# In the loop over pairs of routed tiles, VectorE loads its table behind the products and copies the turned intermediate ahead of the weight copies

## The reference, cut to what matters

```python
# first layer: 32 experts, 4 per token, inner size 192, softmax over the 4 chosen, times 1.8
g = silu(einsum('th,eih->tei', xf, gate_w)); u = einsum('th,eih->tei', xf, up_w)
routed = einsum('tei,ehi,te->th', g * u, down_w, combine)
shared = silu(xf @ shared_gate_w.T) * (xf @ shared_up_w.T) @ shared_down_w.T
# second layer: 8 experts, 2 per token, inner size 176, softmax over all 8
h = silu(einsum('nc,eic->eni', xf, w1)) * einsum('nc,eic->eni', xf, w2)
y = einsum('enc,ne->nc', einsum('eni,eci->enc', h, w3), comb)
sh = silu(xf @ sw1.T) * (xf @ sw2.T) @ sw3.T
```

## Time and profile before

| | us |
|---|---|
| median of 3 runs | 429.84 (426.48 to 432.18) |
| the profiled execution's own time | 427.56 |
| its span in the profile | 425.8 |
| PE busy | 343.6 (81%) |
| DVE busy | 271.4 (64%) |
| ACT busy | 194.0 (46%) |
| POOL busy | 185.0 (43%) |

### The profile page before, as it was taken

The page is one execution under the profiler, slowest core; times in us unless marked ns, Lnnn a source line. Parts: engine busy times, 40 slices in busy tenths (PEclk is TensorE's granted clock), DMA queues, the critical chain, the costliest instruction groups (busy, mean ns, idle before and its releaser), DMA issues.

```text
span 425.8 us, 8440 instructions
## 1 busy us (share of the span) xinstructions
PE 343.6 (81%) x2392; PEld 194.7 (46%) x2392; DVE 271.4 (64%) x842; ACT 194.0 (46%) x452; POOL 185.0 (43%) x321
## 2 busy tenths in 40 slices
PE   0019699768989899898999869999876698885997
PEld 0019564424444444444444558666553344442455
DVE  2997869313666655666555487999777266565174
ACT  1368453243545444454443036999812454540010
POOL 2000001382767766676653217666600657744100
PEclk9999855997999999999999988999976999999899
DMA  7999999085332322333354387920020223321341
GB/s 236 365 223 363 226 351 255 22 261 161 99 100 77 100 87 90 97 85 94 108 164 155 115 340 254 228 67 2 2 97 3 86 75 100 91 74 47 124 151 49
DMA packets 35038, 59.88 MB, mean 141 GB/s; under 512 B 4178, under 2 KB 23346, under 8 KB 34994
## 3 DMA queue, kind: packets, MB, share of 16 engines
q1 hardware_dynamic: 26850, 40.41, 32.4%
q0 software_dynamic: 6528, 17.83, 13.6%
q10 hardware_dynamic: 1616, 1.11, 0.9%
HBM read 47.28 MB, written 12.06 MB: 139 GB/s over the span
## 4 chain that ended last, share of the span: by engine, by line
PE 39%; DVE 26%; issue 14%; DVEq 9%; DMA 5%; POOL 4%; ACT 3%; SPq 0%; ACTq 0%; POOLq 0%
PE bank L1414 8%; DVEq L946 8%; PE bank L1246 6%; PE bank L1426 5%; DVE xn L956 4%; DVE hT L977 4%; DVE dn L957 3%; PE bank L1477 3%; PE bank L1465 3%; PE bank L1159 2%; PE bank L1385 2%; DMA xg<-m_xn,tab 2%; DVE ysb L990 2%; PE bank L1259 2%; DMA x_sb<-x 2%
## 5 line engine op out<-in xcount | busy, mean ns | idle before, releaser
L1385 PE MATMUL bank<-arena,xT 128*64 x272 | 94.7, 492 | 2.4 <-ACT xT L647 2.4
L515 POOL DMA_INDIRECT xg<-m_xn,tab x68 | 66.5, 977 | 65.9 <-PE bank L1367 30.4
L1387 PE MATMUL bank<-xn,xT 128*64 128x384 f32 (+1 forms) x272 | 94.7, 492 | 0.0
L504 POOL DMA_INDIRECT m_ys<-ysb,dest x68 | 71.3, 1049 | 44.3 <-DVE ysb L990 26.6
L636 ACT ACTIVATE xn<-arena 128x768 f32 (+1 forms) x68 | 56.3, 827 | 20.8 <-issue 20.5
L956 DVE COPY xn<-arena 64x256 f32 (+1 forms) x136 | 35.0, 296 | 37.2 <-issue 36.1
L1385 PEld LDWEIGHTS bank<-arena,xT 128*64 128x64 f32 x272 | 35.0, 139 | 44.5 <-issue 43.6
L1414 PE MATMUL bank<-arena,hT 128*64 x136 | 36.4, 390 | 20.2 <-DVE hT L977 20.2
L990 DVE COPY ysb<-bank 128x256 f32<-128x256 f32 x68 | 25.7, 420 | 40.2 <-PE bank L1428 40.2
L647 ACT ACTIVATE xT<-bank 128x512 f32<-128x512 f32 (+1 forms) x36 | 21.3, 591 | 56.1 <-PE bank L1367 56.1
L654 ACT ACTIVATE sg<-bank 128x192 f32<-128x192 f32 (+1 forms) x71 | 22.7, 320 | 39.8 <-PE bank L1387 34.1
(11 more groups left out here) (196 smaller groups left out, 670.2 us busy)
## 6 DMA issues: line engine op xcount, KB each, us to landing
arena<-w_gu SPq DMA_DIRECT2D x3, 3456.0 KB, 21.9
arena<-m_ys SPq DMA_DIRECT2D x8, 512.0 KB, 5.8
arena<-w_dn SPq DMA_DIRECT2D x6, 576.0 KB, 13.8
arena<-w_gu SPq DMA_DIRECT2D x2, 1408.0 KB
arena<-w_dn SPq DMA_DIRECT2D x3, 864.0 KB, 22.3
m_xn<-xn SPq DMA_DIRECT2D x2, 1024.0 KB, 9.6
arena<-m_ys SPq DMA_DIRECT2D x8, 256.0 KB, 3.8
arena<-w_dn SPq DMA_DIRECT2D x7, 192.0 KB, 9.1
```

What stands on the lines that cost most here:

```text
L504: nc.gpsimd.indirect_dma_start(out=ys_d[L.name], out_offset=bass.IndirectOffsetOnAxis(ap=dest[:, s:s + 1], axis=0), in_=ysb[:, s % BUFS, : ...
L515: nc.gpsimd.indirect_dma_start(out=xg[:, b, :], out_offset=None, in_=xn_d[L.name], in_offset=bass.IndirectOffsetOnAxis(ap=d["tab"][:, s:s ...
L1385: T.matmul(out[0:BLOCK, 0:2 * J2], xT[:, s % 4, c, 0:BLOCK], arena[:, bass.ds(off + c * 2 * J2, 2 * J2)], start=(c == 0), stop=(c == C - 1 ...
L1387: ins = T.matmul(out[BLOCK:P, 0:2 * J2], xT[:, s % 4, c, BLOCK:P], gu2[:, s % 2, cols], start=(c == 0), stop=(c == C - 1), tile_position=( ...
```

## The change

Only VectorE's list and one wait of TensorE's are different. In VectorE's list for a pair, `dn_second(p)` was one step with the table load, the six weight copies and their waits, and stood between the output copies and the copy of the intermediate. Now the table load is a step of its own, `experts_of(p)`, directly behind the two products and ahead of the output copies; the copy of the intermediate follows the output copies, and the six weight copies come last, in another order: the two copies that are 128 rows high first, then the four tails. Their one wait on earlier down products is now for both tiles at once. The semaphore `dn_second` counts the two high copies; a new one, `tails_in`, counts the four tails, and TensorE waits for it ahead of the tail products only.

```diff
-                def dn_second(p):
+                def experts_of(p):
                     if 2 * p >= L.tiles:
+                        return None
+                    return nc.values_load_multi_w_load_instructions(
+                        d["etab"][0:1, 4 * p:4 * p + 4], engines=(mybir.EngineType.DVE,), min_val=0, max_val=top)[1]
+
+                def dn_second(p, offs):
+                    if offs is None:
                         return
-                    _, offs = nc.values_load_multi_w_load_instructions(
-                        d["etab"][0:1, 4 * p:4 * p + 4], engines=(mybir.EngineType.DVE,), min_val=0, max_val=top)
-                    for t in range(2):
-                        s = 2 * p + t
-                        if s >= 2:
-                            dve.wait_ge(m["d_done"], s - 1)
-                        if L is L0 and s == late_tile:
-                            dve.wait_ge(w_late, 2 * LOAD)
+                    if p >= 1:
+                        dve.wait_ge(m["d_done"], 2 * p)
+                    if L is L0 and 2 * p <= late_tile < 2 * p + 2:
+                        dve.wait_ge(w_late, 2 * LOAD)
+                    even, even_second, odd, odd_second = offs
+                    V.tensor_copy(dn2[:, 0, :], arena[:, bass.ds(even_second + L.gu, H)]).then_inc(m["dn_second"], 1)
+                    V.tensor_copy(dn2[:, 1, :], arena[:, bass.ds(odd_second + L.gu, H)]).then_inc(m["dn_second"], 1)
+                    for t, b, off in ((0, 0, even), (0, 1, even_second), (1, 0, odd), (1, 1, odd_second)):
                         r = slice(t * BLOCK, t * BLOCK + L.tail)
-                        for b in range(2):
-                            V.tensor_copy(tails[r, b, :], arena[r, bass.ds(offs[2 * t + b] + L.gu + H, H)])
-                        V.tensor_copy(dn2[:, t, :], arena[:, bass.ds(offs[2 * t + 1] + L.gu, H)]).then_inc(m["dn_second"], 1)
+                        V.tensor_copy(tails[r, b, :], arena[r, bass.ds(off + L.gu + H, H)]).then_inc(m["tails_in"], 1)
...
                         product(s)
+                    offs = experts_of(p)
                     if p >= 1:
                         y_copy(2 * p - 2)
                         y_copy(2 * p - 1)
-                    dn_second(p)
                     ht_copy(p)
+                    dn_second(p, offs)
...
+                    if 2 * p < L.tiles:
+                        pe.wait_ge(m["tails_in"], 4 * (p + 1))
```

More of the change, by code:

```diff
@@ L271, in mk_xattn_ffn @@
             m = {n: sem(f"{L.name}_{n}") for n in (
-                "xn_ready xn_stored rt_T rt_Tsb logits exp_in exp_out onehots t_done xT_copied gu_second dn_second g_done "
+                "xn_ready xn_stored rt_T rt_Tsb logits exp_in exp_out onehots t_done xT_copied gu_second dn_second tails_in g_done "
                 "sg_ready h_ready ht_done hT_copied d_done y_copied ").split()}
```

## The result

The changed kernel takes 401.02 us (median of 4 runs, 398.99 to 402.18) against 428.89 for the kernel before (4 runs); ratio 0.934 with a 95% interval of 0.926 to 0.942. Run again beside later kernels it was at 0.941 (0.936 to 0.946), 400.99 us. The forecast was 406 us with a range of 400 to 413. The profiled execution took 402.18 us with a span of 400.4 (before 427.56 and 425.8).

The account below looks back on a forecast made before the run. TensorE was nearly the bound, losing 0.53 us a plain pair waiting for VectorE's turned intermediate. Gains 14.0 + 5.4 + 2.0 + 1.6 = 23.0 take 427.56 to 404.6; median forecast 406 us, range 400 to 413.

Parts of the forecast that it names:

- first network, 23 steps: Time between starts of down products in the first network falls from 5.81 to 5.20 us a pair, 14.0 us in all.
- second network, 8 steps: Time between starts of down products in the second network falls from 5.68 to 5.0 us a pair, 5.4 in all.
- clock behind it: Behind the second network's last step TensorE's lower granted clock costs 1.6 us; with a shorter wait, that is gone.
- Parts 1 and 2: Table load ahead of output copies, half hidden; intermediate ahead of weight copies: together they remove TensorE's hole of 0.53 us a pair.
- The ring: Before the change, down products, then VectorE's output copies, load, weight copies, intermediate and hand-over, 5.68 us from end to end.
- Part 3: VectorE's own work per pair after the change: 4.75 us, under TensorE's 5.16, so VectorE holds nobody.
- rival A: VectorE stays the bound, at 5.35 us a pair in both networks: 411 us; chance 0.15.
- Part 4: TensorE's own table loads could fill its hole instead; costed at nothing, since gate-and-up matmuls hide them.
- rival C: No change to tell: a masked wait, nearest TensorE's table loads, fills the hole; steps stay 5.7, 424 us; chance 0.04.
- Part 5: GpSimd's gathers and stores take 5.22 us a pair, a hair above TensorE's 5.16; first network's step taken as 5.20.
- Rival B: GpSimd becomes the bound once its lag uses up the output buffers' 2 us: 410.5 to 415 us; chance 0.2.
- Rival D: Slower: VectorE's six copies and GpSimd's transfers shut each other out at the port, 7.8 us a pair, 493 us; chance 0.03.

## Why the prediction was right, and where its sizes were off

The sum against the profiled execution was 23.0 us; measured are 25.4. The median came out 5.0 under the 406: 2.4 are those of the sum, the other 2.6 are spread of the runs (I had put the median 1.4 above the profiled execution, and it lies 1.2 below), no mechanism. So 401.0 is inside the range of 400 to 413, but under the 403 to 409 that I gave to the forecast alone. The sum by its own terms:

| term | forecast | measured |
|---|---|---|
| first network, 23 steps | 14.0 | 16.5 (133.66 - 117.21) |
| second network, 8 steps | 5.4 | 6.8 (45.41 - 38.66) |
| its last step | 2.0 | 1.9 |
| clock behind it | 1.6 | 1.6 (tail 32.07 to 30.51) |
| before, and between the networks | 0 | 1.6 - 2.9 = -1.3 |

**Parts 1 and 2** hold in mechanism and in size: the output copies start 0.6 behind the down products' end (forecast 0.55), the intermediate and all copies are there by 3.45 (forecast 3.5), TensorE starts its down products where its own queue would have them. Each move alone gives 70% or more of the gain. The ring was 0.7 to 0.85 longer than TensorE's own step of 5.10 and 4.83. The intermediate ahead of the copies takes out more than that, and the steps are TensorE's own. The load behind the products takes 0.96 out and puts back some 0.56, by which the output copies start later, so its steps stay at 5.15 to 5.20 in most pairs. (The trace before has steps of 5.69, 5.69, 6.17 and 5.87 in turn: two in four are long, not the one that I read. The sum goes by the total and is not touched.)

**Part 3**, VectorE's ring, was mis-sized: 4.75 against 3.3 to 4.3, 3.8 on average. I had put the load's 1.62 behind the product in full; with VectorE late, 0, 0.37 or 0.90 of it were bare in the pairs shown. The slack is about 1.3 us and not 0.35, and **rival A**, against which that slack was my only point, was less likely than I said. The forecast didn't turn on it.

**Part 4** is right: there is no hole in 80 us, and TensorE's table loads start at 200.1 and 200.8, under gate-and-up matmuls that last until 202.8. They cost nothing, and **rival C** is out by it:

```profile
L1358 PEldq TENSOR_LOAD <-etab x2: 301/302/302, 200.1 to 200.8; - x2
```

**Part 5** had GpSimd's pace right and its effect wrong. Its round is 5.17 on average, near the 5.20 that I took. But a GpSimd that falls 0.07 a pair behind does not set the step as long as its lead of two pairs lasts, and it outlasts the stage: TensorE goes at its own step. I had said so myself and still took GpSimd's pace; no row asked for it. TensorE's own step is 5.10, not 5.16: the down products run 0.96 from the first to the tails (202.66 to 203.62) where they ran 1.01, since a first pair of weights is loaded ahead (at 202.34, in the pair of the earlier trace rows at 207.35, right at the first down product). These two are the 2.5 us of the first term. In the second network the step is 4.89 where rows are turned beside it, and 4.45 in the eighth, where none are left to turn; I had 5.0 for all eight. That is the second term.

**Rival B** shows once: beside loads of the next layer's context, issued at 200.66 and 201.65, a store of 200.65 needed 5.70 us to land (2.7 is the median of the earlier trace rows), and the second output copy waited for it 1.12 us:

```profile
206.44 0.42 DVE L992 COPY ysb<-bank 128x256 f32<-128x256 f32 x1 [1.12 <-DMA m_ys<-ysb,dest]
```

The down products of that pair start at 207.76, 5.10 behind the last, by VectorE's slack. But its tail copies end only at 208.73, and the next step is 5.28.

**Rival D**, and the rule that two engines share one pair of ports under an exclusive lock (the Trainium skill, SBUF — State Buffer, "Who interferes with whom"): the four tail copies from 201.65 to 202.65 run for 0.7 us beside the store of 201.94 to 202.98, and the two high copies beside the one of 200.65. One copy takes 0.47 for 0.28, the store 1.04 for 0.99. By the rule as worded one of the two would have stood still for the other, up to 0.7 us; the measurement decides, and it shows delays of 0.05 to 0.2 us. Nothing in these runs tells whether a store needs the ports for a part of its time alone.

**The clock** term was the boldest, and holds. What TensorE did before, in these runs, one trace each: after waits of 2.17, 2.44, 2.59, 3.50 and twice 3.63 us at that place the granted clock is at the lower level for some us; after 1.00 to 1.68 (six traces) it stays full. The length of the wait does not tell the loss: the tail is 1.6 to 1.7 us longer after 2.17, 3.50 and one 3.63, and 3.0 longer after 2.44, 2.59 and the other 3.63 (the kernel with neither move).

**Outside the stages** 1.3 us were lost, in two parts that are not the change's. The start of the first down products, 1.6 earlier here, lies between 98.6 and 102.7 us in the traces, whatever the edit. The stretch between the networks (106.7 before, 109.6 after) goes with the granted clock in the 12 us ahead of the second network's first down products: in six traces it is 0.86 or less there and the stretch is 108.5 to 110.7 us, in the other seven it is 1.00 and the stretch is 106.0 to 107.1. Both traces of the change are among the six, the trace before among the seven, and the edits of the experiments stand on both sides. So the 2.9 us lost between the networks go with the clock. Why an execution gets the one or the other stays open.

## What to carry to other kernels

Find the ring, add up its members, and compare the sum with what the engine that should be the bound needs for itself: the gain is that difference, however much more is taken out. Two moves that each take out most of the difference don't add up, so test them apart before either is kept for its own sake. And where an engine's queue can run ahead, price a register load by what is seen ahead of the next instruction when the engine is late, not when it waits. A helper engine that is slower than the bound by a few hundredths of a us a step does not set the step as long as its lead lasts: multiply the lag by the number of steps before taking its pace.

## What was not expected of the hardware

A table load of four values with its register arithmetic takes 1.5 us in VectorE's queue (198.2 to 199.7), yet only 0, 0.37 or 0.90 of it were bare where the engine had 1 to 1.6 us of work queued. And a short wait of TensorE can cost more than itself: in the one trace with 2.17 instead of 1.68 us of it, the tail behind was 1.7 us longer, at the lower clock.
